# Cross-attention and feed-forward in int8 steps: transposes by DMA, row tiles of 128 across batches, listed orders

## The reference, cut to what matters

```
x1  = x  + w8a8(attention(w8a8(layernorm(x), wq, bq), ctx @ wk.T + bk, ctx @ wv.T + bv, mask), wo, bo)
out = x1 + ffn(layernorm(x1))

w8a8(a, w, b):   sa = max(rowmax|a| / 127, 1e-8);  qa = round(a / sa)
                 sw = max(rowmax|w| / 127, 1e-8);  qw = round(w / sw)
                 (qa @ qw.T) * (sa * sw) + b
attention:       per batch and head (16 heads of width 32): softmax(q k.T / sqrt(32) + mask) v
ffn(a):          qa = round(a * 127 / rowmax|a|), qW1 = round(W1 * 127 / max|W1|)
                 h = gelu(qa @ qW1.T * scales + B1)
                 qh = round(h * 127 / rowmax|h|), qW2 = round(W2 * 127 / max|W2|)
                 qh @ qW2.T * scales + B2
```

## Time and profile before

| | |
|---|---|
| median of 3 runs | 771.72 us |
| the profiled execution, its own time | 769.71 us |
| its span (first to last instruction) | 767.9 us |
| mean granted TensorE clock | 0.967 |
| TensorE busy (matmul) | 669.3 us, 87% |
| VectorE busy | 559.8 us, 73% |
| ScalarE busy | 445.3 us, 58% |
| GpSimd busy | 293.5 us, 38% |
| DMA queue q1 | 24608 packets, 44.38 MB, 18.8% of 16 engines |

### The profile page before, as it was taken

The page is one execution under the profiler, slowest core; times in us unless marked ns, Lnnn a source line. Parts: engine busy times, 40 slices in busy tenths (PEclk is TensorE's granted clock), DMA queues, the critical chain, the costliest instruction groups (busy, mean ns, idle before and its releaser), DMA issues.

```text
span 767.9 us, 15796 instructions
## 1 busy us (share of the span) xinstructions
PE 669.3 (87%) x5576; PEld 517.3 (67%) x5576; DVE 559.8 (73%) x1270; ACT 445.3 (58%) x1084; POOL 293.5 (38%) x538
## 2 busy tenths in 40 slices
PE   0366989999999999999999999999999999997744
PEld 0255767777786777777777777786777777774522
DVE  2788675777878696869687777878696868677554
ACT  2312555666666675757666666666675757565501
POOL 1135152524344353535352524344353535231211
PEclk9998898999999999999999999999999999998778
DMA  9526641020302011121111020202011120000000
...
DMA packets 24684, 45.38 MB, mean 59 GB/s; under 512 B 2144, under 2 KB 12128, under 8 KB 23984
## 3 DMA queue, kind: packets, MB, share of 16 engines
q1 hardware_dynamic: 24608, 44.38, 18.8%
...
## 4 chain that ended last, share of the span: by engine, by line
PE 78%; ACT 8%; DVE 6%; issue 4%; DMA 2%; POOL 2%; SPq 0%; POOLq 0%; DVEq 0%
PE ps_ring L797 30%; PE ps_t L827 13%; PE ps_ring L879 8%; PE ps_ring L897 7%; PE ps_s L820 7%; PE ps_t L839 6%; ACT L498 3%; PE ps_ring L866 2%; ACT pT L506 2%; PE ps_ring L790 2%; DMA pT<-in_wvT 1%; ACT probs L498 1%; PE ps_ring L886 1%; PE ps_ring L849 1%; ACT k_sb L485 1%
## 5 line engine op out<-in xcount | busy, mean ns | idle before, releaser
L506 ACT ACTIVATE pT<-ps_t 125x336 f32<-125x336 f32 x256 | 115.2, 450 | 169.1 <-PE ps_t L827 163.5
L498 ACT ACTIVATE probs<-probs,neg_max 112x375 f32<-112x375 f32 x256 | 153.2, 601 | 14.7 <-DVE neg_max L634 14.5
L827 PEld LDWEIGHTS ps_t<-ident,probs 112*125 112x125 f32 x768 | 112.8, 192 | 72.1 <-issue 38.2
L827 PE MATMUL ps_t<-ident,probs 112*125 112x112 f32 x768 | 132.8, 282 | 26.4 <-ACT probs L498 15.8
L634 DVE CUSTOM_DVE_ANT_0 probs<-ps_s,mask_in 112x375 f32<-112x375 f32 x256 | 130.6, 544 | 28.5 <-PE ps_s L820 21.4
L422 POOL TENSOR_TENSOR ctx_lo<-ctx_in,ctx_hi 128x376 fp32r<-128x376 f32 x64 | 66.0, 1035 | 90.5 <-ACT ctx_hi L480 90.4
L797 PE MATMUL ps_ring<-ctx_hi,wk_hi 128*128 128x376 f32 x256 | 92.6, 362 | 0.0
L797 PE MATMUL ps_ring<-wv_hi,ctx_hi 128*125 128x512 f32 x192 | 82.2, 428 | 8.3 <-POOL ctx_lo L422 8.3
L797 PE MATMUL ps_ring<-ctx_lo,wk_hi 128*128 128x376 f32 x256 | 86.1, 336 | 0.0
L797 PE MATMUL ps_ring<-ctx_hi,wk_lo 128*128 128x376 f32 x256 | 86.1, 336 | 0.0
L797 PE MATMUL ps_ring<-wv_hi,ctx_lo 128*125 128x512 f32 x192 | 77.6, 404 | 0.0
...
## 6 DMA issues: line engine op xcount, KB each, us to landing
ctx_in<-in_ctxT SPq DMA_DIRECT2D x32, 375.0 KB, 3.6
h<-in_w2T SPq DMA_DIRECT2D x4, 1024.0 KB, 5.4
b_row<-in_w2T SPq DMA_DIRECT2D x4, 1024.0 KB, 5.3
x_in<-in_x SPq DMA_DIRECT2D x16, 224.0 KB, 2.6
xres<-in_x SPq DMA_DIRECT2D x16, 224.0 KB, 2.6
out<-y SPq DMA_DIRECT2D x16, 224.0 KB, 3.6
...
w_q<-in_w1T SPq DMA_DIRECT2D x2, 1024.0 KB, 14.8
```

The lines of the kernel that those rows point to most:

```text
L498: nc.scalar.activation(probs[:, hd % SP_RING, :], probs[:, hd % SP_RING, :], ACT.Exp, scale=-1.0, bias=neg_max[:, b % 2, hd:hd + 1], accum ...
L506: nc.scalar.activation(pT[0:LR, hd % PT_RING, :], ps_t[0:LR, 0:LC * N], ACT.Copy).then_inc(pT_s, 1)
L827: last = nc.tensor.transpose(ps_t[0:LR, lc * N:(lc + 1) * N], probs[:, hd % SP_RING, lc * LR:(lc + 1) * LR], ident[0:N, 0:N])
```

## The change

1. *Transposes by DMA.* `x_T`, `o_T`, `y_T` and `h_T` leave TensorE and VectorE. SP issues a DMA with `transpose=True` from the bf16 rows in SBUF to the transposed tile in SBUF, one each for `x_T`, `o_T`, `y_T` (112 or 128 rows x 512) and two for `h_T` (128 x 1024). The row scales of x go out to DRAM (`xs_out`, 112 numbers) and come back spread over all partitions (`xs_in`).
2. *Row tiles.* Output projection and feed-forward run on 14 tiles of 128 rows of the 1792, not on 16 batches of 112. `oT` holds 256 columns, `PV` on ScalarE writes one or two pieces, the row sums are moved to the tile's partitions by small DMAs (`r_move`). Tile t begins when batch t + 1 + t // 7 has its PV.
3. *Weight preparation as units.* The prologues become units (`w_hi`, `w_lo`, `w_rows`, `w_T`, `w_evac`, `so`, `w_load`) that stand in the lists; wk and wv come in halves. The waits for them stand in front of the first use, not ahead of everything.
4. *Listed orders.* The slot pattern is replaced by one list per engine for the whole run, in which each unit stands with its batch or tile and its index (`T 7.2` is head 2 of batch 7, `up 4.0` the first piece of tile 4). The order of units on every engine is thus another, and differs from batch to batch.
5. `q_f` shares memory with `xn`, the zero padding of `ctx_in` is one column, the staging buffers of the weights are others.

```diff
 def turns(order):
     out = []
-    for slot in range(FIRST_SLOT, LAST_SLOT + 1):
-        for name, i, shift in order:
-            b = slot + shift
-            if 0 <= b < (2 if name == "prepare" else B):
-                out.append((name, b, i))
+    for word in order.split():
+        if word[0].isalpha():
+            name = word
+        else:
+            n, i = word.split(".")
+            out.append((name, int(n), int(i)))
     return out
+TILES = B * N // P
+def last_batch(t):
+    return t + 1 + t // 7
+def pieces(b, width):
+    out, r = [], 0
+    while r < N:
+        at = b * N + r
+        n = min(N - r, width - at % width)
+        out.append((r, n, at % width, at // width))
+        r += n
+    return out
 ...
+            def xs_out(b, i):
+                sp.wait_ge(x_s_s, b + 1)
+                wait_for(sp, xs_in_s, 16 * (b - 1))
+                sp.dma_start(q_dram[b % 2, 0, 0, :].rearrange("(n a) -> n a", a=1), x_s).then_inc(xs_out_s, 16)
+            def xs_in(b, i):
+                sp.wait_ge(xs_out_s, 16 * (b + 1))
+                wait_for(sp, q_mul, b)
+                sp.dma_start(xs_bc[:], q_dram[b % 2, 0, 0, :].partition_broadcast(P)).then_inc(xs_in_s, 16)
+            def x_T(b, i):
+                sp.wait_ge(x_quant_s, b + 1)
+                wait_for(sp, q_pe, b)
+                sp.dma_start(xT[:, :, :], x_q[:], transpose=True).then_inc(xT_s, 16)
+            def r_move(b, i):
+                sp.wait_ge(exp_s, 16 * (b + 1))
+                for r, n, at, t in pieces(b, P):
+                    wait_for(sp, r_sum_s, t - 1)
+                    sp.dma_start(rs_in[at:at + n, t % 2, :], row_sum[r:r + n, b % 2, :]).then_inc(rs_in_s[t % 2], 16)
+            def o_T(t, i):
+                sp.wait_ge(o_quant_s, t + 1)
+                wait_for(sp, op_pe, t)
+                sp.dma_start(oqT[:, :, :], o_q[:], transpose=True).then_inc(oqT_s, 16)
+            def y_T(t, i):
+                sp.wait_ge(y_quant_s, t + 1)
+                wait_for(sp, up_pe, 4 * t)
+                sp.dma_start(yqT[:, :, :], o_q[:], transpose=True).then_inc(yqT_s, 16)
+            def h_T(t, i):
+                sp.wait_ge((h_quant_lo, h_quant_s)[i], t + 1)
+                wait_for(sp, down_pe, t)
+                sp.dma_start(hT[:, 8 * i:8 * i + 8, :], h_q[:, i * F // 2:(i + 1) * F // 2], transpose=True).then_inc(hT_s, 16)
 ...
             def PV(b, g):
                 act.wait_ge(pv_pe, 4 * b + g + 1)
                 if g == 0:
-                    wait_for(act, gather_pe, b)
-                nc.scalar.activation(oT[:, g, :], ps_o, ACT.Copy).then_inc(oT_s, 1)
+                    wait_for(act, gather_pe, ((b + 1) * N - 1 - OT) // P + 1)
+                for r, n, at, _ in pieces(b, OT):
+                    nc.scalar.activation(oT[:, g, at:at + n], ps_o[:, r:r + n], ACT.Copy).then_inc(oT_s, 1)
 ...
-            def x_T(b, i):
-                bank = bank_of("x_T", b, 0)
-                dve.wait_ge(xT_pe, b + 1)
-                wait_for(dve, q_pe, b)
-                nc.vector.tensor_copy(xT[:, :, :].rearrange("p k n -> p (k n)"), bank[:, 0:KC * N // 2].bitcast(BF16)).then_inc(xT_s, 1)
-                wait_for(dve, q_mul, b)
-                nc.vector.tensor_copy(xs_bc[:], bank[:, 256:256 + N]).then_inc(xs_s, 1)
 ...
             def down(b, i):
                 if i == 0:
-                    pe.wait_ge(hT_s, 2 * b + 2)
+                    pe.wait_ge(hT_s, 32 * (b + 1))
                     pe.wait_ge(w_quant, 8)
```

More of the change, by code:

```diff
@@ L47 @@
-ACT_UNITS = (
[6 rows of a table removed]
[L54 to L63, removed]
@@ new lines @@
+xs_in 3.0 prepare 1.10 o_T 0.0 xres_load 1.0 prepare 1.12 x_T 3.0 y_T 0.0 x_load 5.0 xs_out 4.0 r_move 2.0 ctx_load 5.0 mask_load
+4.0 h_T 0.0 0.1 o_T 1.0 xs_in 4.0 down 0.3 ctx_load 5.1 xres_load 2.0 x_T 4.0 y_T 1.0 r_move 3.0 mask_load 5.0 x_load 6.0 ctx_load
+6.0 6.1 h_T 1.0 1.1 xs_out 5.0 o_T 2.0 xs_in 5.0 down 1.3 xres_load 3.0 x_T 5.0 y_T 2.0 x_load 7.0 xs_out 6.0 ctx_load 7.0 r_move
+4.0 mask_load 6.0 h_T 2.0 2.1 o_T 3.0 xs_in 6.0 ctx_load 7.1 xres_load 4.0 x_T 6.0 y_T 3.0 x_load 8.0 mask_load 7.0 r_move 5.0
@@ new lines @@
+xs_out 7.0 down 2.3 h_T 3.0 3.1 ctx_load 8.0 xs_in 7.0 ctx_load 8.1 o_T 4.0 xres_load 5.0 x_T 7.0 y_T 4.0 x_load 9.0 xs_out 8.0
+r_move 6.0 down 3.3 ctx_load 9.0 h_T 4.0 4.1 xs_in 8.0 ctx_load 9.1 o_T 5.0 x_T 8.0 mask_load 8.0 y_T 5.0 x_load 10.0 r_move 7.0
+xs_out 9.0 down 4.3 mask_load 9.0 ctx_load 10.0 xres_load 6.0 h_T 5.0 5.1 xs_in 9.0 ctx_load 10.1 o_T 6.0 xres_load 7.0 x_T 9.0
+y_T 6.0 x_load 11.0 x_T 10.0 xs_out 10.0 down 5.3 mask_load 10.0 r_move 8.0 h_T 6.0 6.1 xs_in 10.0 ctx_load 11.0 11.1 down 6.3
@@ new lines @@
+x_load 12.0 mask_load 11.0 xs_out 11.0 r_move 9.0 xs_in 11.0 ctx_load 12.0 12.1 o_T 7.0 xres_load 8.0 x_T 11.0 y_T 7.0 x_load 13.0
+mask_load 12.0 r_move 10.0 xs_out 12.0 ctx_load 13.0 h_T 7.0 7.1 xs_in 12.0 ctx_load 13.1 o_T 8.0 x_T 12.0 y_T 8.0 down 7.3 x_load
+14.0 xres_load 9.0 xs_out 13.0 r_move 11.0 ctx_load 14.0 h_T 8.0 8.1 xs_in 13.0 mask_load 13.0 o_T 9.0 ctx_load 14.1 xres_load
+10.0 x_T 13.0 y_T 9.0 x_load 15.0 r_move 12.0 down 8.3 h_T 9.0 9.1 xs_out 14.0 ctx_load 15.0 xs_in 14.0 ctx_load 15.1 mask_load
@@ new lines @@
+14.0 o_T 10.0 xres_load 11.0 x_T 14.0 down 9.3 y_T 10.0 r_move 13.0 h_T 10.0 xs_out 15.0 h_T 10.1 xs_in 15.0 mask_load 15.0 o_T
+11.0 down 10.3 xres_load 12.0 x_T 15.0 y_T 11.0 r_move 14.0 h_T 11.0 11.1 o_T 12.0 xres_load 13.0 y_T 12.0 r_move 15.0 h_T 12.0
+12.1 down 11.3 o_T 13.0 down 12.3 y_T 13.0 h_T 13.0 13.1 down 13.3
+"""
+POOL_UNITS = """
+x_norm 0.0 split 0.0 0.1 0.2 0.3 x_quant 0.0 x_norm 1.0 q 0.0 split 1.0 1.1 1.2 x_quant 1.0 split 1.3 prepare 0.4 x_norm 2.0 split
+2.0 q 1.0 split 2.1 2.2 x_quant 2.0 split 2.3 x_norm 3.0 split 3.0 prepare 1.4 q 2.0 split 3.1 3.2 3.3 residual 0.0 split 4.0
@@ L88 @@
 RING_USES = [use for use in turns(PE_UNITS)
-             if use[0] in ("x_T", "q", "k", "v", "gather", "o_T", "out_proj", "y_T", "up", "h_T") or use[0] == "down" and use[2] == 0]
+             if use[0] in ("w_T", "so", "q", "k", "v", "gather", "out_proj", "up") or use[0] == "down" and use[2] == 0]
 RING_AT = {use: n for n, use in enumerate(RING_USES)}
@@ L92, with moves_of_tile @@
 ATT_AT = {use: n for n, use in enumerate(ATT_USES)}
+def pieces(b, width):
[6 more added lines that the diff above has]
+    return out
+OT = 2 * P
+OT_DONE = [sum(len(pieces(a, OT)) for a in range(b)) for b in range(B + 1)]
+MOVES = [(b, t) for b in range(B) for _, _, _, t in pieces(b, P)]
+def moves_of_tile(t):
+    return sum(1 for _, a in MOVES if a <= t and a % 2 == t % 2)
 def run(eng, units, order):
@@ L235, in xattn_ffn_kernel @@
         gather_pe = sem("gather_pe")
+        rs_in_s = [sem(f"rs_in_s{i}") for i in range(2)]
         r_sum_s = sem("r_sum_s")
@@ L495, in S @@
                 act.wait_ge(masked, 16 * b + hd + 1)
-                if hd == 0:
-                    wait_for(act, r_sum_s, b - 1)
+                if hd == 0 and b >= 2:
+                    for _, _, _, t in pieces(b - 2, P):
+                        act.wait_ge(rs_in_s[t % 2], 16 * sum(1 for a, c in MOVES if a <= b - 2 and c <= t and c % 2 == t % 2))
                 nc.scalar.activation(probs[:, hd % SP_RING, :], probs[:, hd % SP_RING, :], ACT.Exp, scale=-1.0,
@@ L878, in up @@
                 for k in range(KC):
[L879 removed]
+                    last = nc.tensor.matmul(bank, yqT[:, k, :], w1_q[:, k, j * C:(j + 1) * C], start=(k == 0), stop=(k == KC - 1))
                 last.then_inc(up_pe, 1)
[L882 to L888 removed]
             def down(b, i):
                 if i == 0:
[L892 removed]
+                    pe.wait_ge(hT_s, 32 * (b + 1))
                     pe.wait_ge(w_quant, 8)
@@ L896, in down @@
                     k = 4 * i + n
-                    last = nc.tensor.matmul(bank[0:N, :], hT[:, k, :], w2_q[:, k, :], start=(k == 0), stop=(k == FK - 1))
+                    last = nc.tensor.matmul(bank, hT[:, k, :], w2_q[:, k, :], start=(k == 0), stop=(k == FK - 1))
                 if i == 3:
                     last.then_inc(down_pe, 1)
-            units = {"x_T": x_T, "q": q, "k": k_unit, "v": v_unit, "S": S, "T": T, "PV": PV, "gather": gather, "o_T": o_T,
-                     "out_proj": out_proj, "y_T": y_T, "up": up, "h_T": h_T, "down": down}
+            units = {"w_T": w_T, "so": so, "q": q, "k": k_unit, "v": v_unit, "S": S, "T": T, "PV": PV, "gather": gather,
+                     "out_proj": out_proj, "up": up, "down": down}
             run(pe, units, PE_UNITS)
```

552 lines of the change are left out of this document (328 added, 224 removed), and 12 rows, old and new, of tables (ACT_UNITS, PE_UNITS).

## The result

The changed kernel takes 781.23 us (median of 15 runs, 772.29 to 794.81), the kernel before 772.27 (15 runs on the same chips, 770.41 to 773.75). The ratio is 1.0075, with a 95% interval of 1.0049 to 1.0101: slower by 0.75%, where I forecast 703 and gave "slower" 0.12. The range, 672 to 755, misses it. The ratio rests on the eight shorter of the 15 runs (772.29 to 781.23), and the profiled run, 786.44 us with a span of 784.6, is one of the seven longer ones, so a few microseconds of what follows are its own.

The account below looks back on a forecast made before the run. TensorE's order was taken as the bound from about 80 to 698 us, chains of waits at both ends. 50 + 67 + 407 + 98 + 26 + 45 + 6.5 = 699 us of span, forecast 703, range 672 to 755.

Parts of the forecast that it names:

- start to T 0.4: Start of the kernel: first v product at about 20 us, steady pattern from 50 us instead of 80.
- slots 0 and 1: First two slots, without a tile: 2 x 31.3 us plus 4 us for preparing W1 and W2, ending at 117.
- 13 middle slots, with the lateness of 6.5: Slots 2 to 14: 407 us, plus 98 for 11.5 tiles, plus 6.5 for late transposing DMAs.
- T 15.4 to the end: Last slot 26 us, then 45 us from the last gather, including +5 for transposes becoming DMAs.
- The round trips: Two DRAM trips and batch 0's q transpose, about 3 us each, hidden by v and k; uncovered, 6 us.
- rival A: Inside slots T waits for exp and the bank, so TensorE no longer bounds; tile slots stay 41.2, 722 us; chance 0.17.
- All of this is beside TensorE: Steady slots: changed VectorE, ScalarE and GpSimd work costs nothing; VectorE has 9.5 us to spare, ScalarE 13.9.
- 1.18 us of idle: TensorE's idle time in each old steady slot of 41.17 us, kept in the forecast with and without a tile.
- The lateness of the transposing DMAs: TensorE's waits before out_proj, up and down: 3 us landing, 0.5 us late per tile, 13 x 0.5 = 6.5 us.
- rival C: Transposing DMAs late at out_proj, up and down: lateness x 13 tiles, up to 917 us; chance 0.15, about 0.12 above 772.
- The bare slots: Slots without a tile: 39.8 less 8.5 us of tile work, 31.3 us each.
- rival B: Preparation of weights holds the first batches, VectorE nearly full until 117: 20 us lost, 719 us; chance 0.13.

Follow-up runs that it names:

- e1: Changed kernel with the row scales of x spread by TensorE's diagonal product again, without the DRAM write and read: 754.91 us, ratio 0.980 to the kernel before.
- e12: e1 with a constant weight block in place of the transposed rows of o, y, h, and identity for GELU: 711.40 us, ratio 0.923 to the kernel before.
- e8: Changed kernel with the scales' write directly before its read in SP's list, nothing issued until it lands: 788.49 us, ratio 1.021 to the kernel before.
- e3: Kernel before plus one unread write of 112 x 4 bytes to DRAM ahead of each batch's context loads: 789.61 us, ratio 1.025 to the kernel before.
- e7: e1 with the DMAs of o, y and h copying the same bytes without transposing: 751.25 us, ratio 0.974 to the kernel before.
- e6: e1 with down beginning when the first half of h has landed, two semaphores for one: 750.40 us, ratio 0.974 to the kernel before.

## Why the prediction was wrong

The likeliest case gave 703; three terms failed, and a fourth was near in number. The forecast counts its stretches from head 4 of a batch (T x.4). Counted so by ScalarE's copies in the traces, in us:

| stretch | forecast | after | e1 | e12 |
|---|---|---|---|---|
| start to T 0.4 | 50 | 56.5 | 52.5 | 52.2 |
| slots 0 and 1 | 67 | 90.0 | 81.7 | 82.6 |
| 13 middle slots, with the lateness of 6.5 | 511.5 | 562.1 | 546.0 | 526.2 |
| T 15.4 to the end | 71 | 76.1 | 68.8 | 49.9 |
| span | 699.5 | 784.6 | 749.1 | 710.9 |

**The round trips, priced in the start alone (+21 to +26, in every stretch).** The sentence that failed is "two round trips through DRAM and a transposing DMA for batch 0's q, about 3 us each, which v and k (16 us) hide". I priced them as latency beside other work in one place and gave the 14 others nothing. Each write takes 5.8 us or more to land (e8), in which loads behind it crawl (e3), or transposes and SP's list wait. My bounds for a transfer came from loads in pieces of 1,500 bytes and more; no row showed an element of 4 bytes to DRAM, and I did not give it an upper bound of its own.

**The middle slots and ScalarE (rival A's place, +12 in its waits).** "All of this is beside TensorE" failed for ScalarE. The forecast kept the old slot's 1.18 us of idle, 15.3 in 13 slots, and nearly all of that was TensorE waiting for ScalarE. In the changed kernel these waits are 27.7. Its share was low, but in the timeline above one long piece (GELU and a table, 2.3 us and more) between two copies of probabilities stops T, whose single bank hands over from copy to copy. That the transposes and the diagonal product filled such holes before is argued, not shown; I had seen one of them, the h_T half inside a wait for ScalarE's copy, and kept 0.5 us for it. The 21 us that the tables are worth in e12 are not an error of the forecast in full, since they cost the kernel before 11 us, which its terms hold.

**The lateness of the transposing DMAs (rival C's place).** The landing of 3 us was right (2.4 for the 512-wide ones, 3.2 for half of h in e1, with the pair at 4.6 from the first issue). With the write gone the middle's waits are 6.0, as the 6.5 of the sum, and the end takes 68.8 for 71, so this term was well sized by itself. With the write they are 21.4 in the middle, and the end takes 76.1: what I left out is that another small DMA in the same queue makes them late. The low clock behind the waits adds to that: from batch 2 to 14 the granted clock is 0.96 in the changed kernel and 0.99 in e1.

The Trainium skill's page Advanced Engine Details and Errata (X-Bar Transpose (TRN2)) has a transposing DMA as fast as a plain one. For the kernel's time e7 and e1 agree within their intervals; for the DMA itself the trace does not, since half of h landed 0.9 us earlier as a copy. The 1309 ns that the Trainium skill gives for each 128 x 128 block on its page VectorE: DVE Perf Modes (The three transpose paths) do not add up over blocks here: four blocks landed in 2.4 us and eight in 3.2.

**The bare slots (part of rival B, +15).** "2 x 31.3, and 4 us" became 36.1 and 45.4 in e6:

```profile
47.10:83.20 36.10, 31.96 (x290) 25.56 (x294) 27.95 (x56) 23.86 (x67) 14.72 (x24) 1.00 0.32 93
83.20:128.60 45.40, 35.87 (x286) 29.16 (x290) 25.49 (x52) 22.59 (x64) 10.90 (x18) 0.89 0.54 185
```

Busy time was near in slot 0 (31.96, where 31.3 less the idle kept is 30.1), but subtracting 8.5 us of tile work assumes that nothing else is late without it. Two transposes in a row wait 0.6 us for the copy between them, and 4.1 us of gaps behind ScalarE's copies stand in slot 0. Slot 1 has one gap of 5.2 us at 105. VectorE stands 8 us there for GpSimd's joint maximum of W2 and makes no row maxima for the scores meanwhile; what keeps GpSimd is not shown. The slot pays for it in clock too (0.89):

```profile
DVE s_col L790 <- POOL w_stat L588: 8.0, 1, 8.0
```

**What was right.** The start: first v product at 23.6 us in the changed kernel (20 forecast, 42.8 before) and T 0.4 at 52.5 in e1 (50 forecast, 80 before). A clean slot of 39.9 us. 128 rows at the price of 112: four products of `down` keep 0.86 us on the chain. The end, once the write is gone: 68.8 us. The chance of 0.12 for "slower" had C's mechanism in mind, and the kernel did become slower with TensorE waiting for DMAs, but C laid their lateness to the transposing DMA's own length and to large loads ahead of it; the runs show a small write.

What stays open: e12's middle is 21 us above the 505 of the forecast although it lacks the tables, which the 505 hold. In how far that is the listed order, the low clock (17 us of these slots stand at it) or the waits that e1's product brings (8.1 us) was not separated. The transposes of h back on TensorE, and a later place of `down` in its list, were not tried.
